# A four-layer graph network on one Trainium2 core: the attention score passes gather each tile of edges once into a ring of eight regions, and gathers that no edge needs are left out

## The reference, cut to what matters

```
for _ in range(3):
    x_j = x[src] + edge_attr                 # 80000 x 128: gathered rows plus the edges' own rows
    q = x[dst] @ wq.T + bq ; k = x_j @ wk.T + bk ; v = x_j @ wv.T + bv
    alpha = sum over a head of q * k         # the scores, 4 heads
    a = softmax of alpha over the edges of each dst
    out = segment_sum(a * v, dst)            # then a feed-forward, norms and a GRU cell
```

## Time and profile before

| | us |
|---|---|
| median of three runs | 10036.83 |
| the profiled execution | 9998.96 |
| its span | 9997.1 |
| GpSimd busy in the span | 6270.0 |
| TensorE busy in the span | 6163.4 |
| VectorE busy in the span | 4706.1 |
| three score passes, from first to last gather | 179.1 to 1041.5, 1644.2 to 2513.6, 3115.4 to 3982.4 |
| layer 1 sums and four updates, the same | 4615.0 to 8903.4 |
| layer 3 pass, the same | 9016.1 to 9877.3 |

### The profile page before, as it was taken

How to read it: one execution, slowest core, us unless ns; L and a number is a source line. 1 busy time by engine, 2 the same in 40 slices (tenths; PEclk the granted TensorE clock), 3 DMA queues, 4 the chain that set the end, 5 groups by cost and what they waited for, 6 DMA issues and landing times. The chain is left out here.

```text
span 9997.1 us, 136049 instructions
## 1 busy us (share of the span) xinstructions
PE 6163.4 (62%) x31430; PEld 4983.6 (50%) x31431; DVE 4706.1 (47%) x10319; ACT 1953.8 (20%) x3805; POOL 6270.0 (63%) x6482
## 2 busy tenths in 40 slices
PE   3777676777677777675446445544644554476666
PEld 3666555666555666544444344344434434445554
DVE  5555865555855555944223222322422332246775
ACT  2444124444134444032001000000100000011112
POOL 2777434777325777425774777577577757747774
PEclk7999898999888999886556556655755665588888
DMA  3555432555423554411222222222222222223332
GB/s 85 154 152 153 121 84 72 152 153 152 125 64 90 153 150 147 136 41 49 51 52 65 63 52 64 69 52 52 80 52 52 68 65 52 52 83 105 103 103 65
DMA packets 710785, 908.14 MB, mean 91 GB/s; under 512 B 150464, under 2 KB 450380, under 8 KB 710419
## 3 DMA queue, kind: packets, MB, share of 16 engines
q0 software_dynamic: 198368, 429.61, 16.9%
q1 hardware_dynamic: 489640, 433.13, 14.0%
q10 hardware_dynamic: 22538, 42.81, 1.2%
HBM read 698.72 MB, written 206.25 MB: 91 GB/s over the span
## 5 line engine op out<-in xcount | busy, mean ns | idle before, releaser
L973 POOL DMA_INDIRECT states<-table_typed,tile_idx x2512 | 2436.6, 970 | 1056.3 <-issue 800.4
L956 POOL DMA_INDIRECT states<-table_x,src_idx x2016 | 1988.9, 987 | 729.8 <-issue 622.5
L1060 PE MATMUL psum<-states,select 128*128 x4480 | 1010.9, 403 | 1152.6 <-DVE t L1046 1065.9
L1060 PEld LDWEIGHTS psum<-states,select 128*128 128x128 f32 x4480 | 897.8, 300 | 1277.0 <-issue 1276.7
L1023 DVE SCALAR_TENSOR_TENSOR select<-dst_all,pair_start,iota_row 128x512 f32<-128x512 f32 x560 | 421.4, 752 | 1744.3 <-SPq L1070 1491.4
L1421 PE MATMUL psum<-wt,l_scores_mixT 128*128 128x256 f32 x4032 | 977.2, 386 | 0.0
L1060 PE MATMUL psum<-states,l_update_select 128*128 x2688 | 580.7, 391 | 556.0 <-DVE t L1046 556.0
L978 DVE TENSOR_TENSOR select<-iota_row,dst_local 128x512 f32<-128x512 f32 (+1 forms) x1344 | 858.7, 639 | 95.3 <-issue 55.5
L956 POOL DMA_INDIRECT l_pass_ring<-table_kv,src_idx x672 | 658.1, 979 | 315.8 <-issue 199.5
L1376 DVE TENSOR_TENSOR states<-states 128x512 f32<-128x512 f32 x504 | 350.8, 696 | 1035.5 <-DMA states<-table_x,src_idx 1035.5
L1060 PEld LDWEIGHTS psum<-states,l_update_select 128*128 128x128 f32 x2688 | 518.0, 289 | 624.1 <-issue 624.1
(11 more groups left out here) (371 smaller groups left out, 9695.5 us busy)
## 6 DMA issues: line engine op xcount, KB each, us to landing
states<-in_edge_attr_dram SPq DMA_DIRECT2D x2016, 64.0 KB
rows_dram<-l_scores_values SPq DMA_DIRECT2D x504, 256.0 KB, 2.1
l_values_ring<-rows_dram SPq DMA_DIRECT2D x504, 256.0 KB
table_typed<-states ACTq DMA_DIRECT2D x40, 1024.0 KB, 4.4
states<-table_typed,tile_idx POOLq DMA_INDIRECT x2512
states<-table_x,src_idx POOLq DMA_INDIRECT x2016
table_x<-select SPq DMA_DIRECT2D x50, 256.0 KB, 2.3
l_pass_ring<-table_kv,src_idx POOLq DMA_INDIRECT x672
```

Source lines behind the costliest of these rows:

```text
L956: pool.indirect_dma_start(out=ring[:, k % REGIONS, u, :], out_offset=None, in_=table, in_offset=at).then_inc(gathered[k % REGIONS], 16)
L973: pool.indirect_dma_start(out=ring[:, k % TILE_RING, u, :], out_offset=None, in_=table, in_offset=at).then_inc(gathered[k % REGIONS], 16)
L1060: ins = pe.matmul(psum[:, k % 2, 0:P], picked(more, k)[:, u, :], slots[:, bass.ds(at[u], D)], start=u == 0, stop=u == GROUP - 1)
```

## The change

1. The score pass takes `gathers_by_tile` with the ring of eight, and so 625 gathers where there were 672. The ring lies where ring and attributes lay.
2. The mix becomes four additions of 128x128. Each reads its tile's slot of the ring by an offset from a new table (`mix_plan`: four offsets and the number of the tile region that must have landed, for each region of steps; 20 entries are loaded into registers of VectorE in each turn of the loop). The sum is written over the attributes (`mixed`), no longer into the ring.
3. In this pass GpSimd itself relays the landings (`tells`): before the gathers of region k it waits for the landing of region k - 2 (`TOLD`) and increments `p_landed`; the last two are told after the loop. The room of region k - 8 comes from a second table, `step_room`, against `p_mixed`.
4. The keys are multiplied in place, so ScalarE waits on `p_scored` instead of `p_multiplied`; the values have two buffers instead of four; the loads of the attributes wait on `p_turned` instead of `p_mixed`.
5. `gathers_by_tile` leaves out the three gathers past tile 624 (five passes of layers 1 and 2); `gathers_by_step`, which only layer 3 still uses, stops after 166 regions, leaving out eight gathers.
6. The tables cost six more VectorE operations on one partition and one more DMA in the block that plans the steps.

```diff
+        step_room = sb("step_room", [1, TILE_REGIONS - TILE_RING], I32)
+        mix_plan = sb("mix_plan", [1, STEPS // GROUP, GROUP + 1], I32)
...
+                    sp.dma_start(tile_rows[:], step_row_dram[:]).then_inc(s_in, 16)
...
+                    link(dve.tensor_copy(step_room[:], reach[:, 0:roomy].rearrange("a (g u) -> a g u", u=GROUP)[:, :, GROUP - 1]))
+                    link(dve.tensor_scalar(step_room[:], step_room[:], GROUP.bit_length() - 1, None, ALU.logical_shift_right))
+                    link(dve.tensor_scalar(step_room[:], step_room[:], 1, None, ALU.add))
+                    link(dve.tensor_scalar(mix_plan[:, :, 0:GROUP], rows_by_region, (TILE_RING * GROUP - 1) * P, None, ALU.bitwise_and))
+                    link(dve.tensor_scalar(mix_plan[:, :, GROUP], rows_by_region[:, :, GROUP - 1], (GROUP * P).bit_length() - 1, None,
+                                           ALU.logical_shift_right))
+                    link(dve.tensor_scalar(mix_plan[:, :, GROUP], mix_plan[:, :, GROUP], 1, None, ALU.add))
...
         def gathers_by_step(pool, ring, table, freed):
-            for k in range(STEPS // GROUP):
+            for k in range(EDGE_REGIONS):
...
-        def gathers_by_tile(pool, ring, table, base):
+        def gathers_by_tile(pool, ring, table, base, freed, room, top, tells=False):
             for k in range(TILE_REGIONS):
-                if k >= REGIONS:
+                if tells and k >= TOLD:
+                    pool.wait_ge(gathered[(k - TOLD) % REGIONS], landed((k - TOLD) // REGIONS, base[(k - TOLD) % REGIONS]))
+                    pool.sem_inc(p_landed, 1)
+                elif not tells and k >= REGIONS:
                     pool.wait_ge(gathered[k % REGIONS], landed(k // REGIONS - 1, base[k % REGIONS]))
                     pool.sem_inc(gather_go, 1)
                 if k >= TILE_RING:
...
-                    pool.wait_ge(p_summed, rooms.pop(0))
+                    pool.wait_ge(freed, rooms.pop(0))
                     pool.sem_inc(gather_go, 1)
-                for u in range(GROUP):
+                for u in range(min(GROUP, TILES - k * GROUP)):
...
+            if tells:
+                for k in range(TILE_REGIONS - TOLD, TILE_REGIONS):
+                    r = k % REGIONS
+                    pool.wait_ge(gathered[r], base[r] + TILE_COUNTS[r])
+                    pool.sem_inc(p_landed, 1)
...
         def gat_score_pass(name, base):
-                        gathers_by_step(pool, ring, table_x[:], p_turned)
+                        gathers_by_tile(pool, ring, table_x[:], base, p_mixed, step_room, STEPS // GROUP, tells=True)
...
-                            at_least(sp, p_mixed, region_of(i, r) - (REGIONS - 1))
+                            at_least(sp, p_turned, region_of(i, r) - (REGIONS - 1))
...
-                                at_least(act, p_multiplied, region_of(i, r) - 1)
+                                at_least(act, p_scored, region_of(i, r) - 1)
...
+                        def walks(region, n):
+                            entries = by_step(dve, mix_row, region * (GROUP + 1), n * (GROUP + 1), RING)
+                            return [entries[k * (GROUP + 1):(k + 1) * (GROUP + 1)] for k in range(n)]
...
                             make_select(dve, i, r)
-                            dve.wait_ge(gathered[r], landed(i, base[r]))
+                            dve.wait_ge(p_landed, walk[GROUP].with_bounds(min_val=1, max_val=TILE_REGIONS))
                             dve.wait_ge(p_in[r], (i + 1) * (16 * GROUP))
-                            dve.tensor_tensor(ring[:, r, :, :], ring[:, r, :, :], attr[:, r, :, :], ALU.add).then_inc(p_mixed, 1)
+                            for u in range(GROUP):
+                                at = walk[u].with_bounds(min_val=0, max_val=RING - D)
+                                ins = dve.tensor_tensor(mixed[:, r, u, :], mixed[:, r, u, :], slots[:, bass.ds(at, D)], ALU.add)
+                            ins.then_inc(p_mixed, 1)
```

More of the change, by code:

```diff
@@ L601, in region_of, with step_landed @@
             return i * REGIONS + r
-        ROWS = LOOPS * GROUP * 16
-        TILE_COUNTS = [len(range(r, TILE_REGIONS, REGIONS)) * GROUP * 16 for r in range(REGIONS)]
+        EDGE_REGIONS = -(-(TILES + BLOCKS - 1) // GROUP)
+        assert REGIONS * (LOOPS - 1) + 2 <= EDGE_REGIONS
+        STEP_COUNTS = [len(range(r, EDGE_REGIONS, REGIONS)) * GROUP * 16 for r in range(REGIONS)]
+        TILE_COUNTS = [len(range(r, TILES, REGIONS * GROUP)) * 16 for r in range(REGIONS * GROUP)]
+        TILE_COUNTS = [sum(TILE_COUNTS[r * GROUP:(r + 1) * GROUP]) for r in range(REGIONS)]
         def landed(i, base):
             return base + (i + 1) * (GROUP * 16)
+        def step_landed(i, r, base):
+            return base[r] + STEP_COUNTS[r] if isinstance(i, int) and i == LOOPS - 1 else landed(i, base[r])
         def acc_rows(c, lo, n):
@@ L983, in program @@
         ROOMS_READ = 2 * REGIONS
+        TOLD = 2
+        mix_row = mix_plan[:].rearrange("a g e -> a (g e)")
         sum_row = sum_plan[:].rearrange("a s e -> a (s e)")
@@ L1360, in body @@
                                 act.wait_ge(p_keyed, region_of(i, r) + 1)
[L1361 removed]
+                                at_least(act, p_scored, region_of(i, r) - 1)
                                 act.copy(in_pairs(key[:, r % 2, :, :]), made(r)[:, :, :, 0:D]).then_inc(p_evacuated, 1)
[L1363 to L1365 removed]
+                                if r >= 2:
+                                    act.wait_ge(p_out[r - 2], (i + 1) * 16)
+                                elif not (isinstance(i, int) and i == 0):
+                                    act.wait_ge(p_out[r + 2], i * 16)
+                                act.copy(in_pairs(kept[:, r % 2, :, :]), made(r)[:, :, :, D:2 * D]).then_inc(p_valued, 1)
                         turned(0, 0)
@@ L1385, in body @@
                                 at_least(dve, p_scored, j)
-                                dve.tensor_tensor(in_pairs(prod), in_pairs(key[:, r % 2, :, :]), queries[:, :, :, 0:D],
+                                dve.tensor_tensor(in_pairs(key[:, r % 2, :, :]), in_pairs(key[:, r % 2, :, :]), queries[:, :, :, 0:D],
                                                   ALU.mult).then_inc(p_multiplied, 1)
@@ L1394, in body @@
                                                   queries[:, :, :, D:Q_W], ALU.add).then_inc(p_score_kept, 1)
-                        lead(0, 0)
-                        lead(0, 1)
+                        for r, walk in enumerate(walks(0, 2)):
+                            lead(0, r, walk)
                         turns(dve, body)
@@ L1408, in turn @@
                             for u in range(GROUP):
-                                ins = pe.transpose(psum[:, 1, u * P:(u + 1) * P], ring[:, r, u, :], ident[:])
+                                ins = pe.transpose(psum[:, 1, u * P:(u + 1) * P], mixed[:, r, u, :], ident[:])
                             ins.then_inc(p_turned, 1)
@@ L2173, in program @@
         with nc.Fori(0, GAT_ITERS) as it:
-            gat_score_pass("l0_scores", [it * ROWS] * REGIONS)
+            gat_score_pass("l0_scores", [it * n for n in TILE_COUNTS])
             gat_softmax("l0_softmax")
```

60 lines of the change are left out of this document (31 added, 29 removed).

## The result

The changed kernel takes 10166.53 us (median of 4 runs, 10160.37 to 10168.47), the kernel before, run beside it, 10029.95 (10015.43 to 10039.93): a ratio of 1.0144, 95% interval 1.0130 to 1.0157. I had forecast 9836 us and a faster kernel. It is 1.4% slower, above my range, and not by the train of additions, the slower case that I had named.

What follows compares the result with a forecast made beforehand. GpSimd's gathers were taken to bound the kernel. Per pass 58.6 + 17.9 - 10.5 = 66.0; three passes 198, plus 3, make 201 us: profiled execution 9998.96 to 9798, median 9836, range 9785 to 9945.

Steps and rivals of the forecast that it cites:

- the train of additions: Rival, score pass: VectorE's four additions hold GpSimd's gathers up; each pass loses 63 us, 10223 in all; chance 0.08.
- What bounds the kernel: Score pass: GpSimd is full, gathers following at 1.25 us; long gathers, begun under a select, lose 29.9 us a pass.
- part 1: Score pass, GpSimd: 47 fewer gathers at 1.2475 us save 58.6 us a pass.
- Part 2: Score pass, other engines: VectorE near 3.3 us a region, the chain 3.9, under the gathers' 4.64, so none sets the pace.
- the regions' chain becomes the bound: Rival, score pass: mix to end of queries, about 4.9 us a region, sets the pace; 9902 us; chance 0.15.
- Part 3: GpSimd relaying landings in the score pass: no stall, 3.4 us of reserve; cost 0, bounds 0 and 16 us a pass.
- the hop: GpSimd's relay of a landing to VectorE in the score pass: the mix starts about 0.15 us later.
- Part 4: Score pass: gathers lengthened by VectorE operations lose 12 us a pass instead of 29.9, gaining 17.9; loss bounds 0 and 170.
- the inference that I cited of the Trainium skill: Two-SBUF-input VectorE operations do not stall descriptor writing; rival: long gathers have another source, 9883 us, chance 0.07.
- Part 5: End of a score pass: 20 us from last gather to last multiplication, was 9.5; costs 10.5 a pass, bounds 0 and 15.
- Part 6: Outside the score passes: layer 3 gains 3.7 us, layer 1 gains 1.9, planning loses 2.7; together +3.
- The sum: Whole kernel: 66.0 us a score pass, 198 for three, plus 3: 201 us gained; median forecast 9836 us.

Runs made afterwards that it cites:

- the aligned kernel: Changed kernel with its offset table moved two words, so VectorE's 20-register load starts on a 16-byte boundary, waited-for table values masked: 9822.8 us, ratio 0.9789.
- the AND: Changed kernel with each value loaded from a table and waited for masked with 1023, the control for the other kernels: 10181.8 us, ratio 1.0150.
- the kernel before with the used load: Kernel before plus VectorE's 20-word load, 8 bytes past a boundary, each score-pass turn, one value used: ratios 1.0153, 1.0191, 1.0149; third run 11571.8 us.

## Why the prediction was wrong

*What bounds the kernel, and part 1 (fewer gathers).* Right. 47 gathers fewer a pass; with the load out of the way they follow one another without a stop, 625 in 796.5 us (978.0 + 0.9 - 182.4), within the 785 to 800 that I had given. This holds for the usual chip; on the slower ones they have stops.

*Part 2 (what else could set the pace).* The step that failed: "With registers loaded once in four regions (I take 0.6 to 1.0 us) VectorE stays near 3.3." The load takes 4.88 us, and I had taken the value from no row, though the trace of before had one for 21 registers (4.7 us). The rest of the part was a question of busy time, and 4.9 us of stop are not in it. My first sign of being wrong came with it: GpSimd's gathers pause for room, 39 times in the first pass for more than 0.45 us, up to 5.3. The same part's 3.9 us for the chain holds (4.06 a region, with a load of 1.35 us in each turn). The rival "the regions' chain becomes the bound" was right in kind: but it had 4.9 us a region from a longer train and a hop, and ended faster at 9902; it is 5.4 to 5.5, from a stop once in a turn and a TensorE that starts slowly after it. Only the aligned load tells this from all other parts: it changes nothing else but the AND, and brings the kernel to 9822.8 us, against a forecast of 9836. That closeness is in part luck: I had added 37.9 us because the profiled execution of the kernel before was faster than its median, and the aligned kernel's was not (9824.51). Between the profiled executions the gain is 174 us, between the medians 206, and I had 201.

*Part 3 (the relay).* Right as far as the aligned kernel shows it: where VectorE waits for the tell, its mix starts a median of 1.92 us after the end of the region's last gather (93 pairs in the first pass, one at 3.9), 1.65 before; I had given the hop 0.15, it is 0.27. No gather waited for it. Three readings of the part were off without a consequence for the sum: the mix followed the gather by more than 2.3 us not once but three times (2.4, 3.4 and 3.5); five late pairs of 153 are one in 31, not one in 26; and at 5004.4 GpSimd's sequencer was 11 gathers ahead, under three regions and not four.

*Part 4 (collisions).* About right: 39 gathers longer than 1.1 us in the aligned kernel's first pass, all under a select, where I had said fewer than 30; the time lost in long gathers is 606.33 - 625 x 0.942 = 17.6 us instead of 12. The busy time is GpSimd's, aligned, in this row:
```profile
182.00:999.00 817.00, 638.39 (x4032) 568.44 (x4032) 506.82 (x1341) 360.81 (x672) 606.33 (x625) 0.98 0.54 158
```
So the trace stays with collisions by the select, against the inference that I cited of the Trainium skill (SBUF — State Buffer, Who interferes with whom). The four additions take 0.89 us (I said 0.88), and their train costs GpSimd little: in the aligned kernel's three passes 176 gathers began under it and lost 5.4 us together, while 193 that began under a select lost 46. So that rival falls. The 283 that began under the reduce, which has one input in SBUF, and the 350 under the multiplication, which reads PSUM, lost less than 1 us together. A mix of 512 columns does what the select does: in the kernel before with the used load (the third of its runs) 172 gathers began under it and lost 23 us.

*Part 5 (the end of a pass).* Right with the load aligned: 20.1 us from the last gather's end to the last multiplication (978.9 to 999.0), 20 forecast. In the changed kernel it is 49.5, as VectorE is then some nine regions behind (49.5 / 5.46 us a region).

*Part 6 (the rest)* is small, as I had it: outside the score passes the changed kernel is 2 us shorter than before, where I had 3.

*The sum.* The three passes of the aligned kernel are shorter by 56.3, 62.8 and 59.8 us (816.6, 816.9 and 817.5 from the first gather to the last multiplication), I had 66 each. On average over the three passes every term but one was good to some 6 us; the one that I had waved through was worth 115 to 118 a pass.

## What to carry to other kernels

A load of registers is an operation with a duration, and it stops its engine: look for its row by queue before giving it a number, and count it against the slack at that place of the loop, not against the engine's busy share. Start such a load on a 16-byte boundary. A stop costs more than its length if TensorE falls idle by it, since its next products may run at half speed; and a gain by leaving work out shows only as far as the next chain, here 16.2 us a turn, to which a load of 20 words off its boundary added 5.4.

## What the runs showed of the hardware

- A load of 20 words into VectorE's registers takes 1.35 us from a 16-byte boundary and 4.5 to 4.9 us from 8 bytes past one; ten words take 1.1 and 2.3 us; 21 words 1.6 and 4.7 us, the latter 4, 8 or 12 bytes past it alike; 28 words on a boundary 1.85 us. The long ones come to some 0.07 us a word on, and 0.22 to 0.24 off the boundary.
- After 5.3 us without work TensorE's first eight products took 3.62 us at a granted clock of 0.50, after 1.9 us without work 1.89 us at 1.00.
- A gather that began under a VectorE operation with two inputs in SBUF (select, mix) took up to 1.48 us instead of 0.94; under one that reads PSUM, or the reduce, it took 0.94.
- The same program took 10030 us on one chip and 11398 to 11475 on three others, and the aligned change gained 2.1% on the one and lost 3.5% on the one of the three where it ran.
